# Attention weights times values in eight 64x32 tiles, projection in two column tiles, centred x in SBUF

## The reference

```python
def swin_block_fn(x, shift, mask, ...):            # 8 heads of 8 channels, windows of 7 x 7 = 49 positions
    y = layer_norm(x, ln1_g, ln1_b)
    if shift: y = jnp.roll(y, (-shift, -shift), axis=(1, 2))
    wins = ...                                     # (256 windows, 49, 64)
    qkv = (wins @ qkv_w + qkv_b)...                # q, k, v: (256, 8, 49, 8)
    attn = jnp.einsum('whnd,whmd->whnm', q, k) * hd ** (-0.5) + bias[None] + mask
    attn = jax.nn.softmax(attn, axis=-1)
    out = jnp.einsum('whnm,whmd->whnd', attn, v)...    # weights times values
    out = out @ proj_w + proj_b
    x = x + out                                    # back at its place, rolled back
    z = jax.nn.gelu(layer_norm(x, ln2_g, ln2_b) @ fc1_w + fc1_b, approximate=False)
    return x + (z @ fc2_w + fc2_b)
# twice (shift 0, shift 3), then: covariance of the channels in groups of 16, five Newton steps for its
# inverse root, and the centred x times that 16 x 16 matrix of its group
```

## Time and profile before

| | us |
|---|---|
| median of 3 runs | 833.43 |
| lowest, highest | 830.64, 837.81 |
| the profiled execution's own time | 833.86 |
| its span, first to last instruction | 832.1 |

### The profile page before, as it was taken

The page is one execution under the profiler, slowest core; times in us unless marked ns, Lnnn a source line. Parts: engine busy times, 40 slices in busy tenths (PEclk is TensorE's granted clock), DMA queues, the critical chain, the costliest instruction groups (busy, mean ns, idle before and its releaser), DMA issues.

```text
span 832.1 us, 35518 instructions
## 1 busy us (share of the span) xinstructions
PE 733.5 (88%) x15798; PEld 488.5 (59%) x15798; DVE 520.2 (63%) x917; ACT 360.6 (43%) x628; POOL 202.4 (24%) x503
## 2 busy tenths in 40 slices
PE   3867899999999998999759999999999997999878
PEld 2634676677667765343336676667767653333658
DVE  2643896788677765787555776677667463784123
ACT  1512445445444444675324454444534454574300
POOL 4000022122113101346400221123112111799000
PEclk9967999999999999999978999999999999999959
DMA  9200111112112111000001211112111111000004
GB/s 238 34 20 21 41 58 56 56 56 64 49 52 66 53 47 45 22 1 1 20 21 35 61 57 46 46 55 69 51 55 61 53 32 44 0 2 2 2 19 136
DMA packets 47661, 38.44 MB, mean 46 GB/s; under 512 B 28564, under 2 KB 46996, under 8 KB 47508
## 3 DMA queue, kind: packets, MB, share of 16 engines
q1 hardware_dynamic: 46496, 33.96, 14.2%
q10 hardware_dynamic: 1012, 2.20, 0.8%
HBM read 18.47 MB, written 4.01 MB: 27 GB/s over the span
## 4 chain that ended last, share of the span: by engine, by line
PE 41%; DVE 5%; issue 3%; DMA 1%; ACT 0%; POOL 0%; SPq 0%; DVEq 0%; POOLq 0%; ACTq 0%
PE psum L1017 41%; DVE nmax L805 1%; PE psum L1412 1%; DMA dpk<-osb 1%; DVE lt L784 0%; DVE XW L904 0%; DVE ly L790 0%; DVE lt L783 0%; DVE lt L789 0%; DVE kexp L989 0%; DVE lt L788 0%; DVE ly L786 0%; DVE ly L781 0%; ACT lv L483 0%; DVE kexp L991 0%
## 5 line engine op out<-in xcount | busy, mean ns | idle before, releaser
L415 POOL TENSOR_TENSOR att<-osb,rec 128x392 f32<-128x392 f32 x64 | 70.8, 1107 | 417.4 <-DMA rec<-dens 408.0
L805 DVE TENSOR_REDUCE nmax<-psum 113x16 f32<-113x784 f32 x128 | 118.7, 969 | 83.1 <-PE psum L1017 83.1
L524 ACT ACTIVATE pt<-psum 113x784 f32<-113x784 f32 x128 | 98.6, 822 | 112.6 <-PE psum L1017 110.8
L1017 PE MATMUL psum<-bt,dup_r 113*113 113x392 f32 x256 | 101.0, 394 | 2.6 <-DVE rx L821 1.4
L1017 PE MATMUL psum<-rx,sel_r 128*113 128x392 f32 x256 | 87.7, 343 | 0.0
L1017 PE MATMUL psum<-kexp,qsb 32*49 32x98 f32 x4096 | 71.8, 258 | 8.1 <-issue 7.4
L1017 PEld LDWEIGHTS psum<-kexp,qsb 32*49 32x49 f32 x4096 | 55.9, 121 | 27.2 <-issue 26.2
L1017 PE MATMUL psum<-qexp,ksb 32*49 32x98 f32 x4096 | 68.0, 251 | 0.7 <-issue 0.5
L831 DVE RECIPROCAL rpk<-dpk 64x49 f32<-64x49 f32 x64 | 28.9, 452 | 62.5 <-DMA dpk<-osb 62.4
L1017 PE MATMUL psum<-pt,vbd 113*32 113x49 f32 x4096 | 61.5, 209 | 6.0 <-ACT osb L531 3.1
L1017 PEld LDWEIGHTS psum<-qexp,ksb 32*49 32x49 f32 x4096 | 53.5, 117 | 19.4 <-issue 19.0
(11 more groups left out here) (173 smaller groups left out, 1222.2 us busy)
## 6 DMA issues: line engine op xcount, KB each, us to landing
rec<-dens SPq DMA_DIRECT2D x64, 196.0 KB
kexp<-ksb SPq DMA_DIRECT2D x128, 49.0 KB
qexp<-qsb SPq DMA_DIRECT2D x128, 49.0 KB
XW<-x_dram SPq DMA_DIRECT2D x14, 196.0 KB, 4.8
out_dram<-XW SPq DMA_DIRECT2D x14, 196.0 KB, 2.4
dpk<-osb SPq DMA_DIRECT2D x64, 12.2 KB
dens<-rpk SPq DMA_DIRECT2D x64, 12.2 KB, 2.1
pt<-w_dram ACTq DMA_DIRECT2D x2, 384.0 KB, 6.8
```

What stands on the lines that cost most here:

```text
L415: nc.gpsimd.tensor_tensor(att[:, 4 * part:4 * part + 4, :], osb[part][:, :].rearrange("p (a n) -> p a n", a=4), rec[part][:, :].rearrange( ...
L524: nc.scalar.activation(pt[grp][:, b:b + 2, :], SC[0:KROWS, b:b + 2, 0:BANK], ACT.Exp)\
L805: nc.vector.tensor_reduce(nmax[:, GWIN * grp:GWIN * grp + GWIN, :].rearrange("p w (g a) -> p a w g", g=2)[:, b:b + 2], SC[0:KROWS, b:b + 2 ...
L1017: return nc.tensor.matmul(o, a, b, start=start, stop=stop, **k)
```

## The change

1. *Weights times values.* pv makes one matmul for each window, head **and image**: 64 a call, of 49 rows and 32 columns. The rows of image w are partitions 64w on, so the array is used as eight tiles of 64 x 32. Image 0 goes to bank 4 and image 1 to bank 5. The two head groups `hg` are added up on one column tile: `vbd` is laid out so that the 32 columns read for hg = 0 hold the head's values in columns 0 to 7 and its ones in 8, and those for hg = 1 in 16 to 24, with zeros elsewhere. The output is then 196 columns in each of two banks, in place of 392 in one.
2. *Projection.* `att` is laid out by image, and `proj` makes one matmul for each image, all 128 rows to 64 columns, on two column tiles. Before there were two matmuls of 128 columns, added up.
3. *Values.* `evac_v` is one ScalarE instruction over 113 partitions and no longer two over 49.
4. *Banks.* Bank 5 is now centred x and image 1's output, bank 7 is k, values and projection.
5. *Centred x.* ScalarE copies it out of bank 5 into `z` right after the square, and VectorE multiplies `z` in place.
6. *Waits.* The new semaphore `xc_copied` and the old `osb_done` keep the two uses of bank 5 apart on TensorE: `f_xc_split` waits for the copy of the last output, and `pv` for the copy of centred x.

The core of the diff:

```diff
-        vbd = [sb(f"vbd{i}", [KROWS, WIN * HEADS, 32]) for i in range(2)]
+        vbd = [sb(f"vbd{i}", [KROWS, WIN, 2 * VCOLS]) for i in range(2)]
-        att = sb("att", [128, WIN, NROWS])
+        att = sb("att", [128, 2, WIN, NTOK])
-        bO, bA, bB, bX = PS[4], PS[5], PS[6], PS[7]
-        mF, mY, mV, mW = psum[:, 0:4], PS[4], PS[5], [PS[7], PS[6]]
+        bO, bA, bB, bX = [PS[4], PS[5]], PS[7], PS[6], PS[5]
+        mF, mY, mV, mW = psum[:, 0:4], PS[4], PS[7], [PS[5], PS[6]]
...
                 nc.scalar.activation(sq[:, :], bX[:, 0:TOK], ACT.Square).then_inc(sq_done, 1)
+                if g > 1:
+                    act.wait_ge(v_ready, g - 1)
+                nc.scalar.activation(z[g % 2][:, :], bX[:, 0:TOK], ACT.Copy).then_inc(xc_copied, 1)
...
-                for w in range(2):
-                    nc.scalar.activation(vbd[buf][64 * w:64 * w + NTOK, :, 16 * w:16 * w + HD],
-                                         bA[64 * w:64 * w + NTOK, :].rearrange("p (a d) -> p a d", d=HD),
-                                         ACT.Copy).then_inc(v_done, 1)
+                nc.scalar.activation(vbd[buf][:, :, :].rearrange("p w (g x) -> p (w g) x", g=2)[:, :, 0:128]
+                                     .rearrange("p k (a d) -> p k a d", d=32)[:, :, :, 0:HD],
+                                     bA[0:KROWS, :].rearrange("p (k a d) -> p k a d", a=TILES4, d=HD), ACT.Copy)\
+                    .then_inc(v_done, 1)
...
-                nc.scalar.activation(osb[part][:, :], bO[:, 0:4 * NROWS], ACT.Copy).then_inc(osb_done, 1)
+                nc.scalar.activation(osb[part][:, :].rearrange("p (w n) -> p w n", w=2), psum[:, 4:6, 0:GTOK], ACT.Copy).then_inc(osb_done, 1)
...
-                if not first:
-                    dve.wait_ge(v_ready, g - 1)
-                nc.vector.tensor_tensor(z[buf][:, :], bX[:, 0:TOK], ly[:, :], ALU.mult).then_inc(z_done, 1)
+                dve.wait_ge(xc_copied, g + 1)
+                nc.vector.tensor_tensor(z[buf][:, :], z[buf][:, :], ly[:, :], ALU.mult).then_inc(z_done, 1)
...
                 for win in range(GWIN):
                     for hg in range(2):
                         for h4 in range(TILES4):
-                            c0 = (2 * win + hg) * NTOK
-                            last = mm(bO[32 * h4:32 * h4 + 32, c0:c0 + NTOK],
-                                      vbd[buf][:, (GWIN * grp + win) * HEADS + 4 * hg + h4, :],
-                                      pt[grp][:, h4, c0:c0 + NTOK])
+                            c0, v0 = (2 * win + hg) * NTOK, (VCOLS - 16) * hg + 32 * h4
+                            for w in range(2):
+                                r = slice(64 * w, 64 * w + NTOK)
+                                last = mm(bO[w][32 * h4:32 * h4 + 32, win * NTOK:(win + 1) * NTOK],
+                                          vbd[buf][r, GWIN * grp + win, v0:v0 + 32], pt[grp][r, h4, c0:c0 + NTOK],
+                                          hg == 0, hg == 1)
...
-                for hh in range(2):
-                    last = mm(bank[:, 0:TOK], p["wph"][:, hh, :], att[:, :, hh * NTOK:(hh + 1) * NTOK], hh == 0, hh == 1)
+                for w in range(2):
+                    last = mm(bank[64 * w:64 * w + 64, 0:TOK], p["wph"][:, :], att[:, w])
...
 def step(p, blk, g, u, ahead, tail=None, pair=0):      # TensorE
                 else:
+                    pe.wait_ge(xc_copied, min(G + 3, base + HALVES))
+                    if ahead == 0:
+                        pe.wait_ge(mcopy, 2 * pairs + 2)
                     pv(G - 1, 1, nb)
...
                     else:
+                        pe.wait_ge(osb_done, 2 * G)
                         f_xc_split(blk, g)
...
+                pe.wait_ge(xc_copied, min(G + 4, base + HALVES))
+                if ahead == 0:
+                    pe.wait_ge(mz_done, base + 2)
                 pv(G, 0, u, first and blk == 0)
...
                 pv(G, 1, 1)
+                pe.wait_ge(osb_done, 2 * G + 2)
                 m_xc(2)
```

More of the change, by code:

```diff
@@ L88, in build @@
         gsum = con_view("gsum")
-        perm = [con_view(f"perm{i}") for i in range(2)]
+        perm = con_view("perm")
         fold = con_view("fold", KROWS)
@@ L415, in attn @@
                 nc.gpsimd.tensor_tensor(
-                    att[:, 4 * part:4 * part + 4, :], osb[part][:, :].rearrange("p (a n) -> p a n", a=4),
-                    rec[part][:, :].rearrange("p (a n) -> p a n", a=4), ALU.mult).then_inc(att_done, 1)
+                    att[:, :, GWIN * part:GWIN * part + GWIN, :].rearrange("p w a n -> p w (a n)"),
+                    osb[part][:, :].rearrange("p (w n) -> p w n", w=2),
+                    rec[part][:, :].rearrange("p (w n) -> p w n", w=2), ALU.mult).then_inc(att_done, 1)
             def step(base, g):
@@ L723, in fold_weights @@
                 nc.vector.tensor_scalar(p["wv2"][:, :], raw[:, 2 * CH:3 * CH], v[:, G1:G1 + 1], None, ALU.mult)
-                for w in range(2):
-                    nc.vector.tensor_scalar(p["wph"][:, :, CH * w:CH * w + CH],
-                                            ps[:, CH:3 * CH].rearrange("p (a c) -> p a c", a=2),
-                                            nmask[:, w:w + 1], None, ALU.mult)
+                nc.vector.tensor_copy(p["wph"][:, :], ps[:, CH:2 * CH])
                 dve.wait_ge(s_fold, 2 * k + 2)
-                plink(nc.vector.tensor_tensor(v[:, PB:PB + 1], PS[5 - 5 * k][:, 0:1], v[:, PB:PB + 1], ALU.add))
+                plink(nc.vector.tensor_tensor(v[:, PB:PB + 1], PS[7 - 7 * k][:, 0:1], v[:, PB:PB + 1], ALU.add))
             tlink = chain(tab_link)
@@ L791, in root, with anorm @@
                 assert n[0] == NLINK
-            def anorm(g, buf, after={}, first=False):
+            def anorm(g, buf, after={}):
                 if g:
@@ L872, in _ @@
             dve.wait_ge(s_zero, 1)
+            nc.vector.memset(bA[32:64, :], 0.0)
             widen(0)
             widen(1)
-            anorm(0, 0, first=True)
+            anorm(0, 0)
             dve.wait_ge(s_wide, 2)
@@ L878, in _ @@
             fold_weights(1)
-            anorm(1, 1, first=True)
+            anorm(1, 1)
             table_copies(0)
@@ L1228, in offsets @@
                         mm(ps[r, c:c + 1], raw[r, lo:lo + CH], v[r, off:off + 1])
-                for hh in range(2):
-                    last = mm(ps[:, CH * (1 + hh):CH * (2 + hh)], perm[hh][:, :], raw[:, 3 * CH:4 * CH])
-                last.then_inc(s_fold, 1)
+                mm(ps[:, CH:2 * CH], perm[:, :], raw[:, 3 * CH:4 * CH]).then_inc(s_fold, 1)
                 pe.wait_ge(s_prep, 3 * k + 1)
@@ L1234, in offsets @@
                     r = slice(CH * w, CH * w + CH)
[L1235 removed]
+                    last = mm(PS[7 - 7 * k][r, 0:1], raw[r, 3 * CH:4 * CH], v[r, VB:VB + 1])
                 last.then_inc(s_fold, 1)
@@ L1344, in var_second, with xc_first @@
                     m_var(1)
-                step(p, blk, HALVES - 2, 0, 1, pair=PAIRS - 1, tail=[lambda: m_xc(0), var_first, copied])
+                def xc_first():
+                    pe.wait_ge(osb_done, 2 * G - 2)
+                    m_xc(0)
+                step(p, blk, HALVES - 2, 0, 1, pair=PAIRS - 1, tail=[xc_first, var_first, copied])
                 step(p, blk, HALVES - 1, 1, 0, pair=PAIRS - 1, tail=[xc_second, spread_first, var_second])
                 pv(G, 1, 1)
+                pe.wait_ge(osb_done, 2 * G + 2)
                 m_xc(2)
@@ L1474, in constants @@
     c["turn"], c["both"] = turn, both
-    c["nmask"] = ((np.arange(128)[:, None] % 32 // 16 == np.arange(2)[None]) & (np.arange(128)[:, None] % 16 < HD)).astype(f)
-    for hh in range(2):
-        pm = np.zeros((128, 128), f)
-        for p in range(128):
-            h, dd = divmod(pc[p], HD)
-            if h // 4 == hh:
-                pm[p, 32 * (h % 4) + 16 * pw[p] + dd] = 1
-        c[f"perm{hh}"] = pm
+    pm = np.zeros((128, 128), f)
+    for ch in range(CH):
+        h, dd = divmod(ch, HD)
+        pm[ch, 32 * (h % TILES4) + 16 * (h // TILES4) + dd] = 1
+    c["perm"] = pm
     wm = np.zeros((KROWS, 2), f)
```

39 lines of the change are left out of this document (22 added, 17 removed).

## The result

The changed kernel takes **954.27 us** (median of 4 runs, 948.4 to 957.57) against 835.62 us (4 runs, 830.64 to 845.17) for the kernel before: 1.1435 times as long, 95% interval 1.133 to 1.154. The forecast was 905 us in a range of 850 to 930. Sign and cause of the loss were right, its size was 49 us too small. The profiled execution took 950.99 us, its span is 949.2, so 117.1 us more than before. Executions over 1.5% slower than the fastest of the same kernel are counted in the medians of this document and left out of its ratios.

A forecast was written before the change was run, and what follows sets the result against it. TensorE was taken to run dry at packet ends, one instruction packet each 3.7 us; 256 more records a step add 2.5 us in 28 steps, +70, plus 2 elsewhere: 905 us on the median, range 850 to 930.

The forecast's parts named there:

- Packets of 256 records: TensorE's instruction fetch: each DMA packet holds 256 matmul and load records; 125 packets become 157, 3.7 us a packet.
- one ready ahead: TensorE's instruction queue: about one packet is ready ahead, so a fast packet runs dry before the next arrives.
- R1: Rival: more packets are ready ahead, so only mean supply binds, 16.9 us a step; 850 us, chance 0.10.
- R2: Rival: the fetch stays hidden and array time decides; 841 us, or 866 with pv at 1.7 us; chance 0.07.
- R3: Rival: fetch hidden and eight tiles run pv in the present 0.86 us, leaving the projection's −21 us; 813 us, chance 0.05.
- The new waits: TensorE's waits from sharing bank 5: both cost nothing within the steps; +0.7 us at a block's end.
- the sum that gave 18.6 us a step: Attention step as 4.57 packets: mean of 19.1 and 18.1 us, against 16.1 before; +2.5 us a step, +70 us.
- R4: Rival: the clock drops with the gaps, a fifth of the steps at the lower level; +48 us, 950 us, chance 0.06.
- uniform density: Dense stretch of a step after the change: 1002 records in 10.8 us, taken as 2.8 us for every packet.
- dense run: Small-matmul stretch of a step: scores_t, first pv, scores_t, second pv, f_v, scores; 746 records in 9.95 us before.
- The projection's saving: proj on two column tiles: 1.43 us a call becomes 0.78, −0.65 us for each of 32 calls.
- sparse run: Stretch of f_xc_split, proj, scores, f_var, f_qk, mostly 392-column matmuls; 160 records, 5.47 us before and 4.8 after.

The follow-up runs named there:

- extra_records: Kernel before with a one-column matmul into an unused PSUM column beside each of pv's 32; 964.36 us, ratio 1.1529.
- half_heads: Changed kernel without pv's second head group, 32 matmuls a call instead of 64, half of the heads' output left out; 821.85 us, ratio 0.9817.
- half_projection: Kernel before with the second of proj's two matmuls left out, so half of the heads' contribution missing; 834.56 us, ratio 1.0061.
- twice_projection: half_heads with the matmuls of proj issued twice, the second pair writing the same values; 825.87 us, ratio 0.9943 against the kernel before.
- centred_copy: Kernel before with only the ScalarE copy of centred x into z, where VectorE multiplies it; 825.17 us, ratio 0.9847.
- extra_half: Kernel before with 16 one-column matmuls added in each pv, for the second half of its loop alone; 903.15 us, ratio 1.081.
- fill_half: Changed kernel with one more fp32 matmul of 312 columns, output unused, at the end of each pv; 959.21 us, ratio 1.1471.
- run 65: No run number, but "sparse run" then "65 us": kernel before, 16 one-column matmuls ahead of each f_xc_split, proj, f_var, f_qk; 903.27 us.

## Why the prediction was right or wrong

**Right.** Packets of 256 records, 32 more of them, 157; one ready ahead, 3.7 to 3.9 us each. R1, R2 and R3 are out: extra_records, whose added matmuls have one column, has the full price. The Trainium skill ("Runtime: NRT & Kernel Launch", Instruction fetch mechanics) would have the fetch hidden; in 949.2 us of span TensorE waited 79.3 us for issue, with the gaps at packet ends, and the measurement decides. The new waits (`osb` before `f_xc_split`, pv on the copy of x) cost nothing, as half_heads shows. proj is 0.81 us (200.68 to 201.49), 0.78 forecast. The standing time was forecast as about 3 us a step and is 39.2 / 14 = 2.8, or 3.2 in the steps at full clock.

**The step that failed** is the sum that gave 18.6 us a step, +2.5 over the kernel before, and it failed twice: in its terms at full clock, and in that it had none for the clock. A step at a clock of 1.00 takes 20.06 us and is 3.66 us longer than before, so (3.66 − 2.5) × 28 = **32 us** of the 49 were missed before the clock comes in. All steps together are 4.27 us longer, so the lower clock adds (4.27 − 3.66) × 28 = **17 us**. Both are estimates from five steps of 19.4 to 21.2 us, good to about 9 us either way, and steps with a lower clock may differ in other things too.

*At full clock* standing time grew by 2.45 us a step where the sum has 2.27, and the projection's own work fell by 0.62 where it has 0.65: both right. pv grew by 1.24 where it has 0.88. The operations that the change does not touch grew by some 0.6 where it has nothing. 0.26 of that is bn, which meets VectorE's row maxima now that the projection before it is shorter (below); the small score matmuls have 0.2, and what lengthens them stays open.

*The clock* was set aside as R4 with a chance of 0.06. Its condition came true, but on top of the forecast's mechanism, not in place of it. A mean of 0.91 with two levels means a share s at the lower one with 1 − s / 2 = 0.91: s = 18%, the "fifth of the steps" of R4. I had taken gaps of up to 1.5 us at a clock of 1.00 as leave to sum at full clock with twice as many gaps of up to 2.2 us. Against the earlier trace rows, where a stretch with long waits had 0.76, that was an extrapolation and should have been given a term. The clock and the packets were not rivals: extra_records adds nothing but instructions, and its clock falls to 0.94. That R4's price of 950 us is close to the result is luck: it has 48 us for the clock where some 17 are seen, and the forecast's too short step below it.

**The balance of one block's steps**, forecast against measured: standing still +32 and +27.2; pv busy 0.44 × 28 = +12.3 and +18.8; projection −9.1 and −6.1; all unchanged operations 0 and **+19.3**. Sum: +35 and +59.2. Of the 19.3 some 11 to 13 us are unchanged instructions on a slower clock, as worked out above. Not all of that is lost: the standing time is 2.8 us a step on the mean of all steps and 3.2 in those at full clock, so slower work shortens the waits for packets. How much comes back for each us of slower work is settled by no run.

**pv** was 1.3 us a call in the forecast, bounds 1.0 to 1.7. The calls last 1.31 us from start to next start at the fastest (195.48 to 196.79). They are 0.67 us longer than before on the mean, 18.8 / 28, and 1.24 / 2 = 0.62 at full clock; the forecast said 0.44. The bounds held, the value was low. The other weak term was the *uniform density* of the dense run: a packet that is all pv is used up in 1.5 us, not in the mean 2.8, while another with the 392-column matmuls of scores_t takes longer, and a surplus in the one does not help the other. Yet at full clock standing time came out only 0.2 us a step above the forecast, so this cost little.

**The projection's saving** was counted in full, −0.65 × 32 = −21. half_projection and twice_projection put it between nothing and 10 us: the work hid VectorE's row maxima. The chain "what is late next" was not followed behind this edit.

**Centred x** was costed at nothing, and the first step of a block at +0.4 us. It gains 5 us in each block's first step, 12.8 us on the whole (centred_copy). I had looked only at the steps, where the wait is absent, and not at the page's waits for the whole span, where VectorE's `z` stood with 12.8 us in 3 places, the longest 5.6. This gain hid part of the miss.

## What to carry to other kernels

Count instructions, not only columns: on this kernel 256 more TensorE records a step, laid beside small matmuls, cost 4.2 to 4.4 us a step, so a finer tiling that doubles matmuls of 49 columns loses, and an operand type that halves the records gains. When a forecast adds gaps on TensorE, price them twice, once as gaps and once as clock on everything around them; and to learn which of the two went wrong, compare steps at full clock first. Before counting a saved matmul as time, look what VectorE is finishing behind it; and look for single long waits in the first and last steps, as there a copy that frees a bank can be worth more than a rearranged main loop.

## What the runs showed that I had not expected

- The lower level of the clock came with gaps no longer than 2.2 us (35.7 us of issue waits in 289 us, clock 0.91), and in the changed kernel it sat right behind a gap: 392-column matmuls 0.33 us apart after 191.55, against 0.18, with the granted clock at 0.50 from 191.5 to 194.8.
- The clock was not the larger part of what the forecast missed: steps that never left 1.00 take 20.06 us against 18.6 forecast.
- The cost of records is linear from zero: 838, 903 and 964 us for 0, 128 and 256 more a step. A threshold, which was the rival in extra_half, does not show.
- More work gave a higher clock and no more speed: fill_half at 0.96 takes 959.21 us, the changed kernel at 0.91 takes 954.27.
- 256 more records a step cost 127 us beside pv (964.36 − 837.0), 229 in the sparse run 65 us (903.27 − 837.97).
